# Two graph layers over one 8192 x 8192 adjacency: column 0 used early for both layers, a fixed lead before each row's features, and finished groups that are no longer held back a stage

## The reference

```python
def _L0_gnn_ref(x, adj, u):
    x_drop = x * (u >= 0.1) / 0.9
    return adj @ x_drop
def _L1_gnn_ref(x, adj, kernel, bias):
    x_proj = poincare_expmap(x, 1.0)      # tanh(|x|) * x / (|x| + 1e-8), |x| clipped to 10
    support = adj @ x_proj
    out = poincare_logmap(support, 1.0)   # arctanh(|s|) * s / (|s| + 1e-8), |s| clipped to 0.999
    return out @ kernel + bias
x = _layernorm(x + _L0_gnn_ref(x, adj, L0_gnn_u))
x = _layernorm(x + _L1_gnn_ref(x, adj, L1_gnn_kernel, L1_gnn_bias))
```

## Time and profile before

| | us |
|---|---|
| median of 3 runs | 965.38 (965.21 to 965.78) |
| profiled execution, device time | 965.09 |
| its span | 963.0 |
| TensorE busy | 909.6 (94%) |
| VectorE busy | 318.6 (33%) |
| adjacency read | 330 loads of 1 MB |

### The profile page before, as it was taken

How to read it: one execution, slowest core, us unless ns; L and a number is a source line. 1 busy time by engine, 2 the same in 40 slices (tenths; PEclk the granted TensorE clock), 3 DMA queues, 4 the chain that set the end, 5 groups by cost and what they waited for, 6 DMA issues and landing times.

```text
span 963.0 us, 10566 instructions
## 1 busy us (share of the span) xinstructions
PE 909.6 (94%) x4224; PEld 305.3 (32%) x4224; DVE 318.6 (33%) x1030; ACT 52.5 (5%) x138; POOL 57.0 (6%) x49
## 2 busy tenths in 40 slices
PE   5678989999999999999999999999999999989993
PEld 1112223233333333333333333333333333334441
DVE  1130422324151514332341313403233033176775
ACT  0000000000000000000000000000000000002333
POOL 0000000000000000000000000000000000002332
PEclk9999999999999999999999999999999999999997
DMA  9999999999989999999599996997989989899970
GB/s 368 413 422 421 422 421 422 394 421 371 424 322 422 361 422 396 417 366 381 207 385 420 357 354 211 377 422 272 411 289 367 393 308 417 325 393 422 422 297 33
DMA packets 52607, 353.11 MB, mean 367 GB/s; under 512 B 6224, under 2 KB 8272, under 8 KB 10320
## 3 DMA queue, kind: packets, MB, share of 16 engines
q1 hardware_dynamic: 49824, 350.25, 90.9%
q10 hardware_dynamic: 2736, 2.20, 0.7%
HBM read 350.32 MB, written 2.10 MB: 366 GB/s over the span
## 4 chain that ended last, share of the span: by engine, by line
PE 79%; DMA 13%; SPq 3%; DVE 2%; ACT 1%; issue 1%; POOL 0%; ACTq 0%; POOLq 0%; DVEq 0%
PE sums_both L534 41%; PE sums_part L515 22%; PE sums_first L515 15%; DMA ring<-adj_dram 13%; SPq L269 2%; PE sums_both L564 1%; ACT xres L320 1%; PE sums_first L564 1%; SPq L264 1%; DVE stats L379 0%; POOL rooted L286 0%; DVE y L475 0%; SPq L265 0%; DVE mv L382 0%; DVE feats L475 0%
## 5 line engine op out<-in xcount | busy, mean ns | idle before, releaser
L534 PE MATMUL sums_both<-ring,feats 128*64 128x512 f32 x1920 | 418.4, 592 | 2.8 <-DMA ring<-adj_dram 2.7
L515 PE MATMUL sums_first<-ring,feats 128*64 128x512 f32 x1088 | 250.2, 603 | 32.2 <-DMA ring<-adj_dram 31.9
L515 PE MATMUL sums_part<-ring,feats 128*64 128x512 f32 x1088 | 239.9, 596 | 3.4 <-issue 3.4
L534 PEld LDWEIGHTS sums_both<-ring,feats 128*64 128x64 f32 x1920 | 137.4, 137 | 278.8 <-issue 270.7
L515 PEld LDWEIGHTS sums_first<-ring,feats 128*64 128x64 f32 x1088 | 75.8, 138 | 200.4 <-issue 133.5
L389 DVE TENSOR_TENSOR row_saved<-sums_both,row_saved 64x512 f32<-64x512 f32 x15 | 10.2, 683 | 383.7 <-ACT row_saved L336 383.7
L515 PEld LDWEIGHTS sums_part<-ring,feats 128*64 128x64 f32 x1088 | 78.6, 138 | 155.8 <-issue 154.9
L432 DVE TENSOR_TENSOR support<-sums_part,support 64x512 f32<-64x512 f32 x94 | 64.3, 684 | 137.2 <-PE sums_part L515 136.8
L296 POOL TENSOR_TENSOR rooted<-base,power 128x8 f32<-128x8 f32 x16 | 27.8, 1738 | 820.3 <-DVE base L405 820.3
L433 DVE TENSOR_TENSOR support<-sums_part,support 64x512 f32<-64x512 f32 x95 | 65.9, 694 | 3.3
L336 ACT COPY row_saved<-sums_first 64x512 f32<-64x512 f32 x16 | 9.3, 581 | 700.2 <-PE sums_first L515 700.2
(11 more groups left out here) (51 smaller groups left out, 158.0 us busy)
## 6 DMA issues: line engine op xcount, KB each, us to landing
ring<-adj_dram SPq DMA_DIRECT2D x330, 1024.0 KB, 10.0
xres<-x_dram SPq DMA_DIRECT2D x8, 256.0 KB, 15.9
support<-u_dram SPq DMA_DIRECT2D x8, 256.0 KB, 16.0
out_dram<-xres ACTq DMA_DIRECT2D x16, 128.0 KB, 5.4
selw<-selector_dram ACTq DMA_DIRECT2D x1, 32.0 KB, 3.3
selw<-weight_dram ACTq DMA_DIRECT2D x1, 32.0 KB, 3.7
bias_sb<-bias_dram ACTq DMA_DIRECT2D x1, 32.0 KB, 6.1
```

The lines of the kernel that those rows point to most:

```text
L515: last = nc.tensor.matmul(bank[at:at + F], feats[:, c * TB + t, which, :], ring[:, uses[i][0], t, :], start=start and t < 2, stop=stop and ...
L534: last = nc.tensor.matmul(sums_both[r % 2][layer * F:layer * F + F], feats[:, c * TB + t, layer, :], ring[:, slot, t, :], start=c == 0 and ...
```

## The change

Column 0's blocks of the rows 2 to 15 (kind "early", 14 of them) are used for both layers in row 1's stage, as soon as column 0's features exist, in runs of three among row 1's blocks. Each is a sum of its own in one of two banks, `sums_both0` for even rows and `sums_part3` for odd rows. ScalarE copies the layer-2 half to `support`, VectorE transposes the layer-1 half out of PSUM and adds it to `xres`. The later "both" sums begin with column 1, and VectorE adds them to `support` in the turn, where before ScalarE copied them. Ahead of each column stand blocks worth LEAD = 8 one-layer blocks. The finish steps come every 6 blocks, a row's finish at least two steps behind its last block, pairs are one odd and one even row with interleaved matmuls, and `residual`, `deviation` and `normalise` take group k in step k.

```diff
-TURN_AFTER = 1
-COLUMN_AFTER = 5
-FINISH_EVERY = 5
 GROUP = 2
+LEAD = 8
+EARLY_RUN = 3
+FINISH_EVERY = 6
+FINISH_LAG = 2
...
+    def lead_of(blocks):
+
+        n = work = 0
+        while n < len(blocks) and work < LEAD:
+            work += 2 if blocks[n][0] == "both" else 1
+            n += 1
+        return blocks[:n], blocks[n:]
+
     for r in range(NB):
...
+        holds = [("hold", r, c) for c in range(r + HELD[r] - 1, r - 1, -1)]
+        firsts = [("first", r, c) for c in range(r + HELD[r], NB)]
+        if r == 0:
+            order += firsts + holds + [("turn", 0)]
+            continue
+        lead, rest = lead_of([("both", r, c) for c in range(r >= 2, r - 1)] + firsts)
+        order += lead + column(r - 1) + reread(REREAD[r], r)
+        rest.append(("both", r, r - 1))
+        if r == 1:
+            rest += holds[:-1]
+            early = [("early", row, 0) for row in range(2, NB)]
+            while early:
+                order += early[:EARLY_RUN] + rest[:EARLY_RUN]
+                early, rest = early[EARLY_RUN:], rest[EARLY_RUN:]
+            holds = holds[-1:]
+        order += rest + holds + [("turn", r)]
...
-                    if k:
-                        deviation(k - 1)
+                    deviation(k)
...
+                if step[0] == "early":
+
+                    act.wait_ge(block_released, uses[i][2])
+                    nc.scalar.copy(support[half(r), r // 2], early_banks[r % 2][F:P]).then_inc(early_saved, 1)
...
-                    if k:
-                        normalise(k - 1)
+                    normalise(k)
...
+            def early_end(i, r):
+                rows = slice(r * TB, (r + 1) * TB)
+                dve.wait_ge(block_released, uses[i][2])
+                turn(early_banks[r % 2][0:F].rearrange("p (t n) -> p t n", n=P)).then_inc(early_turned, 1)
+                dve.wait_ge(early_turned, r - 1)
+                done(V.tensor_tensor(xres[:, rows, :], turned[:], xres[:, rows, :], ALU.add))
...
+                if r >= 2:
+                    total = support[half(r), r // 2]
+                    V.tensor_tensor(total, sums_both[r % 2][F:P], total, ALU.add).then_inc(support_begun, 1)
+                    dve.wait_ge(support_begun, r - 1)
                 dve.wait_ge(root_ready, 2 + r + 1)
...
-                    if k:
-                        residual(k - 1)
                     log_scale(k)
+                    residual(k)
...
+                if kind == "early":
+                    if r >= 4:
+                        pe.wait_ge(early_saved, r - 3)
+                        pe.wait_ge(early_turned, r - 3)
+                    pe.wait_ge(mapped, c + 1)
+                    for t in range(TB):
+                        for layer in range(2):
+                            last = nc.tensor.matmul(early_banks[r % 2][layer * F:layer * F + F],
+                                                    feats[:, t, layer, :], ring[:, slot, t, :],
+                                                    start=t == 0, stop=t == TB - 1)
+                    last.then_inc(block_released, 1)
```

More of the change, by code:

```diff
@@ L88, in reread @@
         return steps
-    for r in range(NB):
[L91 to L100, removed]
@@ L103, in work_order @@
-    last = NB - 1
[L104 to L109, removed]
+    def lead_of(blocks):
[4 more added lines that the diff above has]
+        return blocks[:n], blocks[n:]
@@ new lines, in work_order, with group @@
+    last = NB - 1
+    order += reread(LEAD, last) + column(last)
+    rows = sorted((r for r in range(NB) if reread_to[r] < NB), key=lambda r: NB - reread_to[r])
+    ended = {r: 0 for r in range(NB) if reread_to[r] >= NB}
+    waiting = list(ended)
+    since = steps = 0
+    def group(ready, single):
+        for one in ready:
+            for other in ready:
+                if (one - other) % 2:
+                    return one, other
+        return tuple(ready[:1]) if single or len(ready) > 1 else ()
@@ L112, in work_order @@
             order.append(step)
+            steps += 1
             since += 1
[L114 to L117, removed]
-        waiting.append(row)
[L119 to L123, removed]
+            if since >= FINISH_EVERY:
+                ready = [q for q in waiting if steps - ended[q] >= FINISH_LAG]
+                taken = group(ready, row == rows[-1])
+                if taken:
+                    order.append(("finish", taken))
+                    waiting = [q for q in waiting if q not in taken]
+                    since = 0
+        ended[row] = steps
+        waiting.append(row)
+    while waiting:
+        taken = group(waiting[:-1], True) or tuple(waiting)
+        order.append(("finish", taken))
+        waiting = [q for q in waiting if q not in taken]
+    return order
 def place_blocks(order):
@@ L173, in saved_through @@
     def saved_through(r):
[L175 removed]
+        return min(1 + 2 * r, 2 + r)
     with ExitStack() as es:
@@ L328, in _ @@
             k = 0
-            for step in order:
+            for i, step in enumerate(order):
                 r = step[1]
+                if step[0] == "early":
+                    act.wait_ge(block_released, uses[i][2])
+                    nc.scalar.copy(support[half(r), r // 2], early_banks[r % 2][F:P]).then_inc(early_saved, 1)
                 if step[0] == "hold" and step[2] == r:
@@ L393, in layer1_join, with turn @@
                 dve.wait_ge(row_joined, r + 1)
+            def turn(tiles):
+                for f in range(0, F, Q):
+                    for q in range(0, P, Q):
+                        last = V.transpose(turned[q:q + Q, :, f:f + Q], tiles[f:f + Q, :, q:q + Q])
+                return last
+            def early_end(i, r):
[4 more added lines that the diff above has]
+                done(V.tensor_tensor(xres[:, rows, :], turned[:], xres[:, rows, :], ALU.add))
             def layer1_end(r):
@@ L397, in layer1_end @@
                 own = slice(0, TB)
[L398 to L401, removed]
+                done(turn(row_tiles))
                 done(V.tensor_tensor(y[:, own, :], turned[:], xres[:, rows, :], ALU.add))
@@ L488, in _ @@
             for i, step in enumerate(order):
+                if step[0] == "early":
+                    early_end(i, step[1])
                 if step[0] == "hold" and step[2] == step[1]:
@@ L535, in _ @@
                                                     feats[:, c * TB + t, layer, :], ring[:, slot, t, :],
-                                                    start=c == 0 and t == 0, stop=c == r - 1 and t == TB - 1)
+                                                    start=begin and t == 0, stop=c == r - 1 and t == TB - 1)
                     last.then_inc(block_released, 1)
@@ L553, in _ @@
                         pe.wait_ge(part_added, n - PARTS + 1)
+                    if start and n == PARTS - 1:
+                        pe.wait_ge(early_saved, NB - 2)
+                        pe.wait_ge(early_turned, NB - 2)
                     two_halves(sums_part[n % PARTS], 1, i, start, stop).then_inc(block_released, 1)
@@ L561, in _ @@
                         pe.wait_ge(projected_read, finished - 1)
-                    for g, row in enumerate(rows):
-                        for t in range(TB):
+                    for t in range(TB):
+                        for g, row in enumerate(rows):
                             last = nc.tensor.matmul(projected[finished % 2][g][:, t, :],
```

22 lines of the change are left out of this document (15 added, 7 removed).

## The result

The changed kernel takes 981.57 us (median of 4 runs, 981.35 to 982.07) against 965.36 (median of 4) for before on the same chip: a ratio of 1.0168 (95% interval 1.015 to 1.0186), so it is 1.7% slower. The profiled execution has a span of 979.4 us against 963.0. The prediction was 982, with 979.7 for the span.

The account below looks back on a forecast made before the run. Transfers bound the kernel up to 177.64, then TensorE's own work. Gained 16 us ahead of the finish steps, lost 33 to a serial chain of 14.4 us a group: span 979.7, plus 2.1, forecast 982 us, range 977 to 989.

Parts of the forecast that it names:

- Early column: Row 1: fourteen two-unit blocks moved there fill 12.4 us of TensorE idle time; no load wait left after 75.86.
- the 0 to 2 allowed: Ring loads after 75.86: slots that come free late could cost 0 to 2 us, of which 0 was taken.
- the prediction's two lines: Load n lands at 75.86 + 2.482(n - 23); TensorE gets to it at 75.86 + 1.718(units - 23).
- Turn and cover: Row ends: LEAD = 8 covers the 11.8 us turn with 13.7 us, so the stall's 3.4 + 1.9 us go.
- Early blocks on VectorE: Row 1: about 3.0 us a block on VectorE against TensorE's 3.43; no surcharge taken for transposes out of PSUM.
- the prediction's estimate: VectorE in row 1: a PSUM source adds 65 ns a transpose, 0.5 us a block, about 1 us in all.
- First finish step: Start of the finishing part: at 855.9; at equal work 849.0 against 864.98, so 16.0 us gained.
- The serial chain: Finishing part without the held-back stage: each two-row group takes 14.4 us through four engines, over TensorE's 12.0; 33 us lost.
- TensorE's part of a finish step: Finishing part: 1.65 us a step, so a group every 12.0 us; interleaving may shorten it, counted as nothing.
- The finish order, with three groups in a row at the end: End of the finishing part: steps every 6 units, three groups behind TensorE's last part at 925.9; no separate price.
- the rivals: Whole kernel: stages keep TensorE's pace, no change (6%); holding back hid nothing, 949 (4%); early column costs more, 990 (9%).
- The one in which the stages keep TensorE's pace: Finishing part: a group takes under 12.0 us instead of 14.4; device time 965.4 to 965.7, no change; chance 6%.

Follow-up runs that it names:

- The lead alone: The kernel before with LEAD = 8 only, no early column, delay and finish rule of before kept: 967.04 us, 1.0006 of before.
- experiments in both directions: The changed kernel with the one-stage delay put back, 961.43 us; the kernel before with only that delay removed, 992.7 us.
- the third: The changed kernel with ScalarE's squares of group k+1 moved ahead of the normalising of group k: 957.06 us, 0.9904 of before.
- the cures: Two edits to the changed kernel: the one-stage delay put back (961.43 us), or the next group's squares moved ahead on ScalarE (957.06 us).
- the last experiment: Odd and even rows paired in the kernel with early column, lead, delay, before's finish order and squares moved ahead: 950.47 us, against 954.82 without the pairing.
- first and fourth experiment: First: the changed kernel with the one-stage delay put back, 961.43 us; fourth: that kernel with before's order of finish steps too, 955.8 us.

## Why the prediction was right, by its steps

- *Early column.* Right. Hardly a wait for a load is left behind 76 us: 0.7 us idle up to 246.68, inside the 0 to 2 allowed, of which I took 0. The largest, 0.53 us at 246.68, is at the start of row 5's "both" blocks, a place that the prediction had not named. It is load 91, behind 122 units: by the prediction's two lines it lands at 244.6 for a use at 245.9. It landed 2.1 us later than that, so loads 2.482 us apart are not exact enough to say that TensorE is late everywhere.
- *Turn and cover.* Right in the trace: no stall, clock 1.00 up to 856.24. The lead alone shows that this gain by itself doesn't reach the end, a point that the prediction's sum has (it counts the units ahead of the first finish step) but never says.
- *Early blocks on VectorE.* Right: 308 ns a transpose, blocks 3.43 apart. The Trainium skill ("VectorE: DVE Perf Modes", section on the TRN2 errata) gives 120 fixed cycles for a PSUM source and 58 for SBUF, by the prediction's estimate 65 ns; the trace shows a difference of 6 ns, and the trace decides.
- *First finish step.* 855.9 forecast, 856.24 measured. At equal work that is 856.24 - 4 x 1.718 = 849.4, so 15.6 us gained against 16.0.
- *The serial chain.* Right in every term, read between the same instructions as in the earlier trace rows: 5.44 forecast as 5.43 (871.88 to 877.32), 3.80 as 3.81, 1.95 as 1.95, 3.24 as 3.2; 14.43 as 14.4. One-row groups 9.62 against 9.7, the last 11.4 against 11.5. That this chain is the cause is shown by experiments in both directions, and that it closes on ScalarE by the third.
- *TensorE's part of a finish step.* Off: 1.16 and not 1.65 us, since the 1.65 came from a pair whose two rows' matmuls stood one behind the other; interleaved, an odd and an even row take less. So TensorE has a group ready every 11.54 us and not every 12.0. The prediction put the difference beside the chain, at nothing. That holds from the second group on; the first squares stand 1.21 us behind the first finish step (856.24 to 857.45) and not 1.74, so this one step counts, with 0.5 us. Under the cures, where TensorE is the pace, it matters (the last experiment).
- *The finish order, with three groups in a row at the end.* In the sum of the forecast, but not priced by itself. With the delay in place, the change's order costs 5.6 us against before's (first and fourth experiment); what it costs in the changed kernel itself, without the delay, no run shows.
- *The closeness.* The span came 0.3 us under the forecast. Part of that is luck: the first finish step 0.3 late, the first squares 0.5 nearer to it, the seven groups 0.2 longer, the last two 0.2 shorter cancel.

The sum closes: the first finish step comes 8.7 us earlier (864.98 to 856.24), the part behind it is 25.1 us longer (98.0 to 123.2), together 16.4 = 979.4 - 963.0. The chain that ended last runs from 857.45 on through ScalarE, VectorE and GpSimd alone, as forecast. Of the rivals none came. The one in which the stages keep TensorE's pace had 965; with the squares moved ahead they do keep it, and the kernel takes 957, since the last three groups overlap as well.

## What to carry to other kernels

A stage held back by one step costs nothing to look at and can be what lets four engines overlap: before it is removed, add up the chain of one group across all engines and compare it with the time in which the next group arrives. If it is longer, look for the one queue in which the next group's first instruction stands behind this group's last wait; moving that instruction ahead gave back all of the loss here and more. And in this kernel a gain ahead of the closing part counted only as far as it brought that part's first step forward.

## What the runs showed of the hardware

- Sixteen matmul records of 64x128 in a finish step take 1.16 us when the two rows' halves lie on different partitions (one odd, one even row) and their matmuls alternate, and 2.05 when both halves lie on the same. The eight records of a one-row step take 1.16 too, so alternating halves cost no more than one of them. In before, where one row's matmuls all stand ahead of the other's, an odd and even pair took 1.71. All of this is at a granted clock of 1.00.
- In the stall of before, TensorE's granted clock is 0.66 in the 5 us behind 3.38 us of idle time, and 7 blocks take 13.93 us; with the stall gone such a block takes 1.72 us, at 1.00. Behind the waits of 9.8 and 12.4 us in the changed kernel the clock is 0.50, and a one-row finish step takes 2.05 us instead of 1.16.
- A transpose of 32x128 f32 on VectorE takes 308 ns out of PSUM, 302 out of SBUF.
